# A recurrent block with a mixture of experts: taps' row sent second, spreads on 32 rows, idle products ahead of the later W_x products, and a new order of the jobs

## The reference, cut to what matters

```
# branch s: a selective state space layer
xz = rmsnorm(xn) @ W_in;  xi, z = split(xz)          # 256 channels each
xc = silu(conv4(xi) + conv_b)                        # causal, 4 taps, per channel
dt, B, C = split(xc @ W_x, [64, 80])                 # rank 64, 16 states
dt = softplus(dt @ W_dt + b_dt)
h[t] = exp(dt * A) * h[t-1] + (dt * xc) * B          # per channel and state
y = sum_states(h * C) + D_skip * xc
s = xn + (y * silu(z)) @ W_out
# branch moe: 8 experts, each token weighs its best two
score = top2 of softmax(xn @ Wg), normalised
moe = sum_e score_e * (relu(xn @ W1_e + b1_e) @ W2_e + b2_e)
```

## Time and profile before

| | us |
|---|---|
| median of 3 runs | 275.86 |
| the runs | 275.59, 275.86, 277.68 |
| the profiled execution, its own time | 278.05 |
| its span (first to last instruction) | 276.0 |

### The profile page before, as it was taken

The page is one execution under the profiler, slowest core; times in us unless marked ns, Lnnn a source line. Parts: engine busy times, 40 slices in busy tenths (PEclk is TensorE's granted clock), DMA queues, the critical chain, the costliest instruction groups (busy, mean ns, idle before and its releaser), DMA issues. The chain is left out here.

```text
span 276.0 us, 4179 instructions
## 1 busy us (share of the span) xinstructions
PE 252.0 (91%) x1227; PEld 133.2 (48%) x1227; DVE 249.0 (90%) x284; ACT 228.3 (83%) x436; POOL 237.0 (86%) x191
## 2 busy tenths in 40 slices
PE   7889597699999899899999999789999999999992
PEld 7434241274546433445656426237647446566442
DVE  4696999949799999999999999998799999999994
ACT  1589996989979999999789899996788986878560
POOL 5509699739899999879999999977989997999995
PEclk9999999689999999999999999957999999999999
DMA  5987980024490660024670058070399700000002
GB/s 155 234 250 186 224 203 4 7 77 91 93 207 14 148 159 0 2 70 96 134 180 1 0 126 181 2 161 11 80 207 210 191 2 0 2 0 0 2 1 76
DMA packets 18979, 26.16 MB, mean 95 GB/s; under 512 B 6615, under 2 KB 12174, under 8 KB 18958
## 3 DMA queue, kind: packets, MB, share of 16 engines
q1 hardware_dynamic: 18066, 24.71, 38.1%
q10 hardware_dynamic: 700, 0.66, 1.0%
q0 software_dynamic: 192, 0.52, 0.9%
...
## 5 line engine op out<-in xcount | busy, mean ns | idle before, releaser
L445 POOL TENSOR_TENSOR hc<-hs,Ct 128x1024 f32<-128x1024 f32 x63 | 149.3, 2382 | 5.7 <-DMA Ct<-bc_rows 2.0
L951 DVE TENSOR_TENSOR_SCAN hs<-dec,pdbu 128x1024 f32<-128x1024 f32 x62 | 139.4, 2273 | 0.0
L638 ACT ACTIVATE dec<-rep,negA 128x512 f32<-128x512 f32 x124 | 85.0, 724 | 0.3 <-DMA rep<-dt_u 0.2
L927 DVE TENSOR_TENSOR pdbu<-rep,px 128x1024 f32<-128x1024 f32 x60 | 70.9, 1218 | 8.2 <-PE px L1174 8.1
L1200 PEld LDWEIGHTS px<-w,hT 128*128 128x128 f32 x512 | 62.5, 197 | 14.0 <-issue 8.9
L1194 PE MATMUL px<-xnT,w 128*128 128x512 f32 x128 | 64.9, 614 | 2.2 <-DVE pdbu L927 1.3
L1200 PE MATMUL px<-w,hT 128*128 128x128 f32 x512 | 65.7, 284 | 0.2 <-DVE pdbu L927 0.2
L578 POOL TENSOR_TENSOR acc<-acc,ysc 128x512 f32<-128x512 f32 x30 | 38.3, 1276 | 14.8 <-ACT ysc L752 14.8
L763 ACT ACTIVATE hT<-px,cols 128x512 f32<-128x512 f32 x64 | 43.4, 693 | 8.0 <-PE px L1194 5.5
L752 ACT ACTIVATE ysc<-px,score 128x128 f32<-128x128 f32 x120 | 34.0, 367 | 16.7 <-PE px L1200 16.6
L1083 PE MATMUL py<-hc,rsel 128*32 128x512 f32 x252 | 36.1, 619 | 1.7 <-POOL hc L445 1.7
...
(10 more groups left out here) (162 smaller groups left out, 275.9 us busy)
## 6 DMA issues: line engine op xcount, KB each, us to landing
...
```

The source lines that it names most:

```text
L445: eng.tensor_tensor(hc[:, n % HC_RING], hs[:, n % HS_RING], Ct[:, k % 2, j:j + 1, :].to_broadcast([P, 2, CH]), ALU.mult).then_inc(hc_last ...
L638: act.activation(dec[:, n % DEC_RING, i, :], rep[:, q, 0, :], ACT.Exp, scale=negA[:, q, j:j + 1])\
L927: dve.tensor_tensor(pdbu[:, at:at + 2, :], rep[:, 2 * pair:2 * pair + 2, 1, :], B[:, None, :].to_broadcast([P, 2, CH]), ALU.mult).then_inc ...
L951: dve.tensor_tensor_scan(states.rearrange("p b t -> p (b t)"), dec[:, n % DEC_RING].rearrange("p b t -> p (b t)"), pdbu[:, at:at + 2, :].r ...
```

## The change

1. **Fetches.** ScalarE's queue sends the taps' row second, `cw` third. conv_b, b_dt and D_skip go to GpSimd's queue, behind the identity, with a semaphore of their own. SP sends `W_dt` as one transfer, and A_log ahead of the rest of x.
2. **v0 and v1** work on 128 rows: `wdt` is [128, 256] with rows 64 to 127 set to zero by VectorE, and the moving tile is `dtp` whole. ScalarE's second copy (L728) is gone.
3. **Spreads.** `e0`, `e1` and both `spread_u` work on 32 rows (0 to 31 for the first, 32 to 63 for the second) instead of 128, and both `spread_u` stand behind `e1`.
4. **Idle products.** Ahead of each `dt.1`, `dt.2`, `dt.3`: six, into dt's own bank, once it is emptied and ahead of the wait for `xc`.
5. **The order**: `tn` ahead of `v0`, `B1` behind `e1`; nearly all places of `EARLY`, `TABLE`, `STEPS`, `START` and `AHEAD` move by a few slots. VectorE's `times_dt` of chunk 0's second half moves from slot 2 to slot 0.

```diff
-PRE_JOBS = ["tr", "xc0", "xc1", "dt", "v0", "v1", "B0", "B1", "tn", "e0", "e1"]
+PRE_JOBS = ["tr", "xc0", "xc1", "dt", "tn", "v0", "v1", "B0", "e0", "e1", "B1"]
 EARLY = {
-    0: ["gl", "m1b", "m0a", "z0", "z1"], 2: ["m0b", "m1a"], 9: ["gs"], 10: ["gb"],
+    0: ["gl", "m1b", "m0b", "z1"], 1: ["m0a", "z0"], 3: ["m1a"], 9: ["gs"], 10: ["gb"],
 }
...
-AHEAD = [2, 9, 3, 3, 3, 3, 2, 3, 2, 2, 2, 2, 3, 5, 1, 3, 1, 3, 3, 1, 3, 6, 2, 4, 3, 4, 2, 2, 2, 1, 4, 3]
+AHEAD = [2, 9, 4, 3, 4, 2, 2, 4, 0, 2, 2, 1, 2, 3, 1, 3, 0, 3, 5, 1, 3, 3, 2, 3, 4, 3, 2, 2, 2, 2, 2, 3]
...
-BUSY = {"row": 14, "tr": 2, "xc1": 2}
+BUSY = {"dt": 6, "row": 14, "tr": 2, "xc1": 2}
...
-            for b in range(DB):
-                sp.dma_start(wdt[RANK * b:RANK * (b + 1), :], W_dt[:, b * P:(b + 1) * P]).then_inc(w_proj, 16)
-            sp.dma_start(x_sb[:, 1:CHUNKS], ...).then_inc(x_in[2], 16)
+            sp.dma_start(wdt[0:RANK, :], W_dt[:, :]).then_inc(w_proj, 16)
             for i in range(GROUP):
                 sp.dma_start(alog[GD * i:GD * (i + 1)]...).then_inc(w_alog, 16)
+            sp.dma_start(x_sb[:, 1:CHUNKS], ...).then_inc(x_in[2], 16)
...
+            pool.dma_start(rows[V_CB:V_CB + 2, :], conv_b...).then_inc(w_rows_soft, 16)
+            pool.dma_start(rows[V_BDT:V_BDT + 2, :], b_dt...).then_inc(w_rows_soft, 16)
+            pool.dma_start(rows[V_DS:V_DS + 2, :], D_skip...).then_inc(w_rows_soft, 16)
...
-            act.dma_start(cw[:, :, :], ...).then_inc(w_tap, 16)
-            act.dma_start(rows[V_CB:V_CB + 2, :], conv_b...).then_inc(w_rows, 16)
-            act.dma_start(rows[V_BDT:V_BDT + 2, :], b_dt...).then_inc(w_rows, 16)
-            act.dma_start(rows[V_DS:V_DS + 2, :], D_skip...).then_inc(w_rows, 16)
             act.dma_start(hc[:, 0]..., conv_w...partition_broadcast(P)).then_inc(w_row, 16)
+            act.dma_start(cw[:, :, :], ...).then_inc(w_tap, 16)
...
-                    act.activation(dtp[0:RANK + 2 * STATES, :], src[...], ACT.Copy).then_inc(dt_copied, 1)
-                    ins = act.activation(dt_low[:, :], src[0:RANK, :], ACT.Copy)
+                    ins = act.activation(dtp[0:RANK + 2 * STATES, :], src[...], ACT.Copy)
...
+            pe.wait_ge(w_rows_soft, 16 * N_SOFT)
             pe.transpose(pdbu[:, 2, 0:V_END], rows[:, :], ident[0:V_END, 0:V_END]).then_inc(vec_t, 1)
...
-                pe.matmul(pdbu[:, 2 + i, :], copies(i), dt_u[:, 0, 1, :], start=True, stop=True).then_inc(u_spread, 1)
+                pe.matmul(pdbu[:, 2 + i, :], copies(i), dt_u[GD * i:GD * (i + 1), 0, 1, :], start=True, stop=True)\
+                    .then_inc(u_spread, 1)
...
                 elif job == "dt":
                     if k == 0:
                         pe.wait_ge(w_proj, 16 * N_PROJ)
+                    else:
+                        keep_busy(BUSY["dt"], dst)
...
-                    last = pe.matmul(dst[:, :], wdt[RANK * b:RANK * (b + 1), :], (dtp[0:RANK], dt_low)[b],
-                                     start=True, stop=True)
+                    last = pe.matmul(dst[:, :], wdt[:, b * P:(b + 1) * P], dtp[:, :], start=True, stop=True)
...
-                if job in ("e0", "e1"):
-                    spread_u(int(job[1]))
+                if job == "e1":
+                    spread_u(0)
+                    spread_u(1)
```

More of the change, by code:

```diff
@@ L69 @@
 }]
 STEPS = [{
-    "silu": [10], "times_dt": [17, 28], "scale_rows": [0], "normalise": [8],
-    "gate": [19, 19, 21, 21, 22, 23, 25, 25, 25, 26, 26, 29, 30], "gate_e": [16], "gate_p": [27],
-    "gate_y": [22, 38], "far": [18, 28], "third": [16], "taps": [7, 7, 10],
-}, {
-    "silu": [11], "times_dt": [15, 25], "scale_rows": [0], "normalise": [2],
-    "gate": [19, 20, 23, 23, 24, 24, 25, 25, 26, 29, 29, 30, 30], "gate_e": [16], "gate_p": [36], "finish": [31],
-    "gate_y": [21, 38], "far": [20, 33], "third": [17], "taps": [3, 4, 8],
-}, {
-    "silu": [11], "times_dt": [17, 21], "scale_rows": [0], "normalise": [5],
-    "gate": [20, 21, 24, 25, 26, 26, 27, 27, 27, 31, 31, 31, 33], "gate_e": [18], "gate_p": [30], "finish": [11],
-    "gate_y": [22, 37], "far": [20, 22], "third": [17], "taps": [1, 7, 8],
+    "silu": [10], "times_dt": [15, 27], "scale_rows": [1], "normalise": [8],
@@ new lines @@
+    "gate": [19, 19, 21, 21, 22, 22, 23, 23, 23, 24, 25, 25, 27], "gate_e": [16], "gate_p": [25],
+    "gate_y": [22, 38], "far": [15, 30], "third": [15], "taps": [7, 8, 9],
+}, {
+    "silu": [11], "times_dt": [18, 23], "scale_rows": [0], "normalise": [2],
+    "gate": [19, 19, 22, 23, 23, 23, 24, 25, 25, 27, 31, 31, 32], "gate_e": [19], "gate_p": [37], "finish": [32],
+    "gate_y": [20, 38], "far": [19, 31], "third": [18], "taps": [4, 7, 8],
+}, {
+    "silu": [12], "times_dt": [16, 16], "scale_rows": [0], "normalise": [5],
+    "gate": [19, 20, 25, 26, 27, 27, 27, 28, 29, 31, 32, 32, 33], "gate_e": [22], "gate_p": [30], "finish": [12],
+    "gate_y": [23, 38], "far": [16, 20], "third": [18], "taps": [2, 6, 10],
@@ L82 @@
 }, {
-    "gate_y": [20, 43], "last_table": [37],
+    "gate_y": [21, 39], "last_table": [29],
 }]
 START = {
-    "second": [2], "gate": [1, 2, 2, 2, 2, 3, 5, 5, 6, 6, 9, 9, 9], "gate_e": [0], "gate_p": [8], "third": [10],
+    "second": [0], "gate": [1, 2, 2, 2, 3, 3, 4, 4, 4, 4, 5, 5, 8], "gate_e": [0], "gate_p": [7], "third": [9],
 }
-AHEAD = [2, 9, 3, 3, 3, 3, 2, 3, 2, 2, 2, 2, 3, 5, 1, 3, 1, 3, 3, 1, 3, 6, 2, 4, 3, 4, 2, 2, 2, 1, 4, 3]
+AHEAD = [2, 9, 4, 3, 4, 2, 2, 4, 0, 2, 2, 1, 2, 3, 1, 3, 0, 3, 5, 1, 3, 3, 2, 3, 4, 3, 2, 2, 2, 2, 2, 3]
@@ L269, in mamba_moe @@
         N_REP = 16 * 2 * GROUP
-        N_SETUP, N_SELECTED = 2, QUADS + DB + 1
-        N_ROWS, N_PROJ, N_MOE = 5, 4, 3 + TPC
+        N_SETUP, N_SELECTED = 3, QUADS + DB + 1
+        N_ROWS, N_SOFT, N_PROJ, N_MOE = 2, 3, 3, 3 + TPC
         xv_dram = x.rearrange("b (h p) d -> p (b h) d", p=P)
@@ L817, in _ @@
             dve.memset(dtp[RANK + 2 * STATES:P, :], 0.0).then_inc(setup, 1)
+            dve.memset(wdt[RANK:P, :], 0.0).then_inc(setup, 1)
             def stats(g):
@@ L1046, in _, with keep_busy @@
             pe.wait_ge(consts, 4)
-            def keep_busy(count):
+            def keep_busy(count, dst=pdbu[:, 3]):
                 for _ in range(count):
-                    pe.matmul(pdbu[:, 3, 0:P], ident[:, :], ident[:, :], start=True, stop=True)
+                    pe.matmul(dst[:, 0:P], ident[:, :], ident[:, :], start=True, stop=True)
             keep_busy(BUSY["row"])
             pe.wait_ge(w_rows, 16 * N_ROWS)
+            pe.wait_ge(w_rows_soft, 16 * N_SOFT)
             pe.transpose(pdbu[:, 2, 0:V_END], rows[:, :], ident[0:V_END, 0:V_END]).then_inc(vec_t, 1)
@@ L1153, in fill @@
                 elif job in ("v0", "v1"):
-                    pe.wait_ge(dt_copied, k + 1) if job == "v0" else wait_emptied(pe, "dt", k)
+                    wait_emptied(pe, "dt", k)
                     b = int(job[1])
-                    last = pe.matmul(dst[:, :], wdt[RANK * b:RANK * (b + 1), :], (dtp[0:RANK], dt_low)[b],
-                                     start=True, stop=True)
+                    pe.wait_ge(setup, N_SETUP)
+                    last = pe.matmul(dst[:, :], wdt[:, b * P:(b + 1) * P], dtp[:, :], start=True, stop=True)
                 elif job == "gl":
@@ L1178, in fill @@
                     pe.wait_ge(far_done, 1)
-                    last = pe.matmul(dst[:, :], copies(int(job[1])), dt_u[:, 0, 0, :], start=True, stop=True)
+                    q = int(job[1])
+                    last = pe.matmul(dst[:, :], copies(q), dt_u[GD * q:GD * (q + 1), 0, 0, :], start=True, stop=True)
                 elif job == "gs":
```

25 lines of the change are left out of this document (11 added, 14 removed), and 29 rows, old and new, of the table TABLE.

## The result

The changed kernel takes 278.24 us (median of 11 runs), the kernel before 275.86 (11 runs): a ratio of 1.0081, 95% interval 1.0049 to 1.0114. It is slower by 0.8%, where I had forecast 274.1, which is 0.6% faster. Its profiled execution took 278.77 us, so it stands close to its median.

The account below looks back on a forecast made before the run. TensorE was taken as the bound where VectorE waits for a B job, VectorE elsewhere. Start -1.8, chunk 1 +1.8, chunk 2 +0.5 and chunk 3 -2.3 sum to -1.8: 274.1 us by the median, range 270.5 to 279.5.

Parts of the forecast that it names:

- Start: From the first fetches to VectorE's first units: earlier taps' row and overlapping 32-row spreads put steady work 1.8 us ahead.
- v0 and v1: In each chunk: two 128-row products cost TensorE 0.96 us more than the overlapping pair; dropping ScalarE's second copy is worth 0.
- Six idle products: Ahead of dt.1, dt.2, dt.3: 1.6 us of TensorE each, 3.2 at half clock, free if `xc` is not ready.
- Chunk 1's preparation: From gb.0 to B.8: shorter wait at B.4, about 6 us at B.5, clock falls again; +1.8 us.
- Chunk 2's: From B.8 to B.12: 4.3 us more TensorE work nearly cancels against its room; 0 to 1.3, taken as +0.5 us.
- Chunk 3's: Near 180 us: idle products fill gaps, clock stays up, 3.8 us return, less 1.2 at B.20 and 0.3 for v; -2.3 us.
- End: Last steps of GpSimd and VectorE: order kept and nothing waits behind ScalarE's earlier table load; 0 us.
- Rival 3: At the start: rows on GpSimd's queue come late or 32-row products don't overlap, so no gain; 275.9 us, chance 0.12.
- Rival 1: Both clock falls stay, shown by clock 0.50 when B.20 to B.22 are filled; 278.9 us by the median, chance 0.25.

Follow-up runs that it names:

- c5: The changed kernel without idle products at dt and with the three rows on SP's queue: 272.32 us, 0.9891 of the kernel before.
- a4: The changed kernel without any idle products at dt, chunk 0 and later: 273.84 us, 0.9963 of the kernel before.
- a1: The changed kernel with conv_b, b_dt and D_skip on SP's queue instead of GpSimd's: 276.41 us, 1.0052 of the kernel before.
- a3: The changed kernel without the six idle products behind dt of chunk 0, the later ones kept: 276.20 us, 1.0040 of the kernel before.
- b3: The kernel before with spreads on 32 rows, tn ahead of v0 and B1 behind e1: 275.54 us, 0.9986 of the kernel before.
- d3: c5 with v0 and v1 as a pair of 64 rows: 279.02 us, 1.0145 of the kernel before.
- d1: The kernel before with v0 and v1 on 128 rows and nothing else: 276.11 us, 1.0021 of the kernel before.
- b4: The changed kernel with v0 and v1 on 64 rows and ScalarE's second copy back: 279.6 us, 1.0146 of the kernel before.
- c1: The kernel before with only the changed tables (new order, 64-row pair, no idle products): 278.1 us, 1.0085 of the kernel before.
- c3: The kernel before with a new start (taps' row second, rows on SP's queue, A_log early, 32-row spreads, tn and B1 moved): 275.91 us, 0.9998.
- b1: The kernel before with six idle products ahead of dt.1, dt.2 and dt.3 and nothing else: 274.96 us, 0.9960 of the kernel before.
- b2: The kernel before with conv_b, b_dt and D_skip on GpSimd's queue and nothing else: 276.37 us, 0.9989 of the kernel before.
- d2: c3 with v0 and v1 on 128 rows: 274.70 us, 0.9988 of the kernel before.

## Why the prediction was wrong, step by step

The change comes out as three measured steps: the order with the 128-row products and the new start, -1.1% (c5); the rows on GpSimd's queue, +0.7% (a4 against c5); the idle products, +1.2% (the changed kernel against a4). They lead from one kernel to the next, so they have to give the +0.8% in sum; taken the other way round (a1 between c5 and the changed kernel), the idle products are 1.6% and the queue 0.3%. I had the first too small and the other two at almost nothing.

*Start, -1.8 us forecast.* This is the step that failed first. In the trace it is +1.0 us. I had bounded the rows on GpSimd's queue at 0 ("late by as much as is won") and took them as in time, with no row that showed it: they hold the transpose 2.07 us. a1 gives 1.5 us back and c5 shows that it lasts to the end. The second part I did not see at all: the entry in `BUSY` acts at chunk 0 too (a3: up to 0.6 us at unit 1). Reading who else looks the table up would have shown it. What I worked out for the spreads was right in mechanism and size (0.94 us for a pair; unit 1 0.8 us earlier with their order in b3).

*v0 and v1, +0.96 us in each chunk.* In the new order the sign is wrong: d3 puts the pair back and loses 2.5%. In the old order d1 is not told from no change. I had priced ScalarE's second copy at 0, since "in later chunks ScalarE isn't what the B jobs wait for"; in d3's chunk 3 it stands ahead of the pair, and the pair doesn't overlap there. What is not settled is how much of d3's 4.6 us between units 40 and 48 the clock's fall has and what sets it off: all five traces with a fall of 8 us or more there (before, b4, c1, c3, d3) have the pair, and none of the ten with 128 rows; but b1, b2 and b3 have the pair and no such fall, and in two of the five (before and c3) it begins ahead of the pair. That is a correlation, not a cause shown, with one execution for each kernel: two of the twelve executions of d1, and two of d2, have a mean clock of 0.966, below that of their traces (0.984 and 0.972).

*Six idle products, +1.6 us of TensorE each.* The mechanism was right, 1.34 us at full clock (179.35 to 180.69 in the changed kernel) and 2.7 where it was at half. In chunk 1 the difference between the changed kernel and a4 grows by 2.1 us from unit 8 to 16, where 1.6 were forecast; it grows by 1.3 more to unit 24 and is 0.9 above that of unit 16 at unit 40. What was wrong is chunk 3: I let them keep the clock up there. In the old order they do (b1), but a4 and c5 keep it up without them. In the new order they bought nothing and cost 3.3 us in all, the start's part with it.

*Chunk 1's preparation, +1.8 us.* Measured 4.1 beyond the start's 1.0 (3.5 with 1.6 us taken off). The long wait came where I said, ahead of B.5, with 5.0 us (at gl.1) where I had about 6, and that at B.4 went to 1.46. Missing in the sum were the transfer of the thirds (2.16 us of TensorE idle ahead of B.4, with the fall of the clock behind it instead of at gb.0) and a wait of 1.83 us for a decay.

*Chunk 2's, +0.5 us.* Measured 2.1 from unit 16 to 40, the idle products' 0.9 among them.

*Chunk 3's, -2.3 us.* Measured -4.7 between units 40 and 62. Sign and place right, reason wrong, as above. And the 3.8 us that I took back stand in a trace of the dearer kind: the median from which I counted has executions with less time at half level in it.

*End, 0.* From unit 62 to the end all kernels with the new order take 16.3 us and all with the old 15.9: +0.4.

Rival 3 (the start brings nothing) named the mechanism that happened at the start, with 0.13; it put the time at 275.9, since it went no further than the gain. Rival 1 put the time at 278.9, close to the 278.24 measured, but by luck: its condition was a clock at half level when B.20 to B.22 are filled, and the clock is 1.00 from 180 to 200 us. The rule of the Trainium skill (TensorEngine Tiling (Array Packing), Performance Considerations) on row tiles held for the 32-row pairs (0.94 us for two). For v0 and v1 I took a loss from it, and the runs decide against that here: in the new order the pair of chunk 3 does not overlap.
